# Attention in two passes, and the softplus polynomial by its quadratic factors, in a fused decoder layer

## The chip, the cores and the metric

The kernel runs on one core of one Trainium2 chip. The metric is the device time of one execution in microseconds (us). A difference counts here from 0.2% (about 3.3 us) on; the chances of the prediction are given by that bound. A profile is one execution taken by the hardware profiler.

## What is computed

One decoder layer over 4 batches of 512 tokens with 512 features, in fp32, in three parts, each added to the residual `x`:

```python
x = x + attention(layernorm(x))          # 16 query heads, 2 key/value heads, 32 features each, causal, rotary
x = x + mamba(ctx, gate=layernorm(x))    # selective scan, 512 channels, 16 states, z = layernorm(x)
x = x + ffn(layernorm(x))                # 1408 wide, silu gate, router, 8 adapters of rank 16, two chosen
```

The attention is `softmax(q @ k.T * scale, causal) @ v @ wo.T`. The scan, per state `n` of 16, is

```python
dt = softplus(w_dt @ (w_x @ u) + bias)                     # softplus(v) = relu(v) + log1p(exp(-abs(v)))
state = state * exp(dt * A[n]) + (dt * u) * B[n]           # along 512 tokens
y += state * C[n]
```

`log1p(t)` for `t` in 0 to 1 is `t` times a polynomial of degree 9.

## The kernel before, in words

All weights but those of the FFN stay in SBUF. The work of one batch is attention, the scan, then the FFN. The scan of batch t+1 does not depend on the residual, so its pieces are laid beside other work: beside the 33 evaluations of the FFN of batch t (gate and up, 11 tiles of 128 columns, three evaluations each), beside its down projection (11 tiles), and beside the 32 steps of attention of batch t+1. `plan` (L93) fills these slots in order: `PLAN_NEXT` gives the evaluations 30 pieces, the down projection 22 (`IN_DOWN`), attention the last 8. Batch 0 has no FFN before it, so `PLAN_FIRST` puts 13 pieces beside its projections and 47 into its attention. A state of the scan is three VectorE pieces over 128x2048 elements: `mul` (L1086), `run` (the scan itself, L1091) and `out` (L1096). For each state ScalarE makes the decay (four exponentials, L583) and fetches rows B and C (L573), and GpSimd adds the product to `y_sb` by an accumulating DMA (L487):

```python
pool.wait_ge(y_added, 16 * (b * NS + n))     # add n waits for add n-1
dve.wait_ge(y_added, 16 * (b * NS + n - 1))  # mul n (n >= 2) waits for add n-2: two state buffers
```

The softplus polynomial is the first 12 pieces: one TENSOR_SCALAR (L1061), nine SCALAR_TENSOR_TENSOR (L1064, Horner), the sum with relu (L1069), and `dt * u` (L1072).

Down projection (PE, L970 to L974): for each of 11 tiles four matmuls, and `project(b, f)` beside it (L774): in turn the raw q tiles and k (L782), their rotation (L789) and v (L796). `rotate` (L1098) on VectorE makes 3 instructions per tile, 5 tiles. `finish` (L1277) then adds the result out of the four banks of `ps_a`, and only then can attention use these banks.

Attention before has 32 steps: step s is two heads (`pair`) of query tile i (128 queries) against (i+1) key tiles. PE: two matmuls of 32 rows, side by side in the array, and two bf16 mask matmuls (`scores`, L820, L823). VectorE: negated row maxima (L1126). ScalarE: exponentials with bias and row sum (L625). PE: transposes of the probabilities (L834); ScalarE copies them to SBUF (L637). Each two steps make a group of four heads: PE spreads the inverse row sums (L844) and weighs the values (L849, four column tiles of 32 side by side), ScalarE and VectorE move and scale (L644, L1139). So each query tile passes PE, VectorE, ScalarE, PE, ScalarE, PE, ScalarE, VectorE. Two pairs of banks hold the scores: `scores(s)` waits for the exponentials of s-2. The output projection of query tile i (L873, four matmuls) comes at steps 31, 33, 34, 35 (`OUT_AT`). Then VectorE does the first sum (L1172), norm and gate (`gate_stages`, L1142).

Queues: SP loads inputs and FFN weights and stores the output; ScalarE's queue loads B and C; GpSimd's the accumulating DMAs and the small powers of the norms (L477). Matmuls in fp32 show as two records each (two passes), with two weight loads.

## Time and profile before

| | |
|---|---|
| Median of 3 runs | 1651.27 us (1648.47 to 1651.48) |
| Profiled execution: its own time | 1649.75 us |
| Its span, first to last instruction | 1647.9 us |
| Mean granted TensorE clock | 0.876 |
| Busy: PE, VectorE, ScalarE, GpSimd | 1406.0, 1218.4, 604.9, 111.9 us |

1649.75 us is the profiled execution's own time; the span leaves out what lies before the first and after the last instruction. Busy shares are averages over stages. PE's busy time counts matmuls in flight, so it grows when the clock is low.

The period of a batch in steady state is 384 us. In the trace the FFN of batch 0 and the scan of batch 1 lie between 293 and 541 us, the attention of batch 1 from 553.5 us, and so on.

### The profile page before, as it was taken

Reading aid. Unit: us, or ns where it says so; the run is one execution under the profiler, and the core shown is the slowest. Engines: PE = TensorE matmul, PEld = TensorE weight load, DVE = VectorE, ACT = ScalarE, POOL = GpSimd, SP = SyncE. Lnnn points to the kernel's source line nnn. Section 1 sums busy time; section 2 is a strip of 40 time slices with the busy share of each in tenths; the row PEclk is TensorE's granted clock in tenths of the full one; section 3 lists DMA queues with packets and bytes.
Section 4 is the critical chain, followed back from the end, with each engine's and each line's share of the span. In section 5 each row is a group of like instructions: output and inputs, shape, how many; then the busy total and the mean of one; then the engine's idle time right before and its main releaser. Section 6 shows DMA issues by size and latency. Waiting matters only on the chain.

```text
span 1647.9 us, 16148 instructions
## 1 busy us (share of the span) xinstructions
PE 1406.0 (85%) x5768; PEld 685.0 (42%) x5768; DVE 1218.4 (74%) x1411; ACT 604.9 (37%) x1436; POOL 111.9 (7%) x116
## 2 busy tenths in 40 slices
PE   5756767999888799899889699899879788799999
PEld 2333433443333354444334255444334345454434
DVE  4899996589989766759998865759998967623330
ACT  5165553323223584232232376242333267211110
POOL 0000001001100000000110000100210000100000
PEclk8855558999999699899999779899999869789999
DMA  4167761123666631112656822012556741101112
GB/s 185 39 147 153 154 141 27 44 66 108 143 141 166 166 66 26 39 50 78 159 128 159 196 68 52 26 37 84 124 131 152 173 135 27 26 13 64 48 32 83
DMA packets 53278, 158.81 MB, mean 96 GB/s; under 512 B 5072, under 2 KB 10704, under 8 KB 44752
## 3 DMA queue, kind: packets, MB, share of 16 engines
q0 software_dynamic: 9216, 67.11, 19.8%
q1 hardware_dynamic: 25664, 54.23, 9.9%
q10 hardware_dynamic: 18320, 36.45, 8.6%
q8 instruction: 47, 0.77, 0.2%
q14 instruction: 31, 0.25, 0.0%
HBM read 86.20 MB, written 4.46 MB: 55 GB/s over the span
## 4 chain that ended last, share of the span: by engine, by line
DVE 30%; issue 30%; PE 29%; DMA 6%; ACT 4%; POOL 2%; DVEq 0%; ACTq 0%; POOLq 0%
DVE state L1091 11%; DMA y_sb<-state 5%; PE ps_a L894 5%; DVE state L1086 4%; PE ps_a L974 4%; PE ps_a L820 3%; DVE state L1096 3%; PE ps_b L834 3%; PE ps_w L873 3%; PE ps_a L906 3%; POOL rstd L477 2%; PE ps_b L914 2%; PE ps_w L782 2%; ACT r L625 2%; DVE neg_max L1126 2%
## 5 line engine op out<-in xcount | busy, mean ns | idle before, releaser
L894 PE MATMUL ps_a<-xt,w_sb 128*128 128x512 f32 x704 | 319.2, 607 | 0.0
L1091 DVE TENSOR_TENSOR_SCAN state<-decay,state 128x2048 f32<-128x2048 f32 x64 | 282.8, 4418 | 5.3 <-ACT decay L583 0.5
L677 ACT ACTIVATE r<-ps_a 128x512 f32<-128x512 f32 x132 | 78.6, 596 | 380.6 <-PE ps_a L906 202.8
L894 PEld LDWEIGHTS ps_a<-xt,w_sb 128*128 128x128 f32 x704 | 138.1, 197 | 174.9 <-issue 174.9
L820 PE MATMUL ps_a<-r 32*128 32x512 f32 (+3 forms) x512 | 140.4, 634 | 81.7 <-ACT r L625 55.2
L906 PE MATMUL ps_a<-r,wb_sb 128*128 128x512 f32 x352 | 177.1, 628 | 35.9 <-DVE r L1267 33.7
L583 ACT ACTIVATE decay<-dt_sb,decay_rate 128x511 f32<-128x511 f32 x256 | 162.9, 712 | 104.9 <-DVE state L1096 72.2
L1260 DVE SCALAR_TENSOR_TENSOR r<-r,ps_a 128x512 f32<-128x512 f32 x132 | 89.9, 681 | 146.3 <-ACT r L677 146.3
L625 ACT ACTIVATE r<-ps_a,neg_max 128x128 f32<-128x128 f32 (+3 forms) x256 | 133.6, 534 | 116.6 <-DVE neg_max L1126 116.1
L974 PE MATMUL ps_a<-wd_sb,r 128*128 128x512 f32 x352 | 162.4, 613 | 0.0
L1086 DVE TENSOR_TENSOR state<-du_sb,bc_sb 128x2048 f32<-128x2048 f32 x64 | 146.3, 2286 | 4.7 <-DMA y_sb<-state 4.6
L1096 DVE TENSOR_TENSOR state<-state,bc_sb 128x2048 f32<-128x2048 f32 x64 | 145.9, 2280 | 0.7
L834 PE MATMUL ps_b<-cst,r 128*128 128x128 f32 x640 | 121.4, 333 | 26.0 <-ACT xt L637 16.8
L906 PEld LDWEIGHTS ps_a<-r,wb_sb 128*128 128x128 f32 x352 | 67.4, 197 | 131.1 <-issue 124.7
L1126 DVE TENSOR_REDUCE neg_max<-ps_a 128x2 f32<-128x256 f32 (+3 forms) x128 | 104.0, 814 | 21.1 <-PE ps_a L823 20.2
L487 POOL DMA_DIRECT2D y_sb<-state x64 | 56.1, 876 | 752.5 <-DVE state L1096 676.9
L974 PEld LDWEIGHTS ps_a<-wd_sb,r 128*128 128x128 f32 x352 | 70.1, 200 | 88.8 <-issue 86.8
L834 PEld LDWEIGHTS ps_b<-cst,r 128*128 128x128 f32 x640 | 89.9, 174 | 34.7 <-issue 29.5
L914 PE MATMUL ps_b<-r,ad_sb 128*128 128x512 f32 x176 | 89.8, 635 | 13.5 <-DVE r L1267 13.5
L820 PEld LDWEIGHTS ps_a<-r 32*128 32x128 f32 x512 | 49.9, 237 | 118.4 <-ACT r L625 77.2
L1267 DVE TENSOR_TENSOR r<-r,ps_a 128x512 f32<-128x512 f32 x132 | 90.7, 687 | 9.6
L477 POOL TENSOR_TENSOR rstd<-var_eps,cst 128x1 f32<-128x1 f32 x48 | 56.0, 1167 | 576.4 <-DVE var_eps L1024 576.4
(120 smaller groups left out, 1475.7 us busy)
## 6 DMA issues: line engine op xcount, KB each, us to landing
y_sb<-state POOLq DMA_DIRECT2D x64, 1024.0 KB, 9.7
bc_sb<-bc_rows ACTq DMA_DIRECT2D x64, 512.0 KB, 5.1
w_sb<-in_w_tiles SPq DMA_DIRECT2D x44, 512.0 KB, 3.7
wd_sb<-in_w_down SPq DMA_DIRECT2D x44, 256.0 KB, 3.5
wb_sb<-in_w_adapt SPq DMA_DIRECT2D x44, 128.0 KB, 2.1
xa<-in_x SPq DMA_DIRECT2D x4, 1024.0 KB, 5.2
out_x<-xb SPq DMA_DIRECT2D x16, 256.0 KB, 7.0
xn_att<-in_ctx_t SPq DMA_DIRECT2D x4, 512.0 KB, 6.1
```

Source lines behind the costliest of these rows:

```text
L583: nc.scalar.activation(decay[:, n % 2, j, 1:L], dt_sb[:, j, 1:L], ACT.Exp, scale=decay_rate[:, j, n:n + 1]).then_inc(decay_ready, 1)
L625: nc.scalar.activation(probs[:, (2 * s + k) % 4, 0:(i + 1) * P], score_place(s, k), ACT.Exp, bias=neg_max[:, s % 2, k:k + 1], accum_out=ro ...
L820: nc.tensor.matmul(score_place(s, k), q_t[rows, m, i * P:(i + 1) * P], k_t[rows, 0:width], start=True, stop=False, tile_position=(rows.sta ...
L834: mm = nc.tensor.transpose(ps_b[:, k, kt * P:(kt + 1) * P], probs[:, (2 * s + k) % 4, kt * P:(kt + 1) * P], ident)
L894: mm = nc.tensor.matmul(ps_a[:, 2 * (f % 2) + half, :], w_sb[:, slot, at + k * P:at + (k + 1) * P], xt[:, k, :], start=(k == 0), stop=Fals ...
L906: mm = nc.tensor.matmul(ps_a[:, 2 * (f % 2) + half, :], wb_sb[:, f % 2, at:at + P], low[:, 2 * half + k - 1, :], start=False, stop=(k == 2 ...
L914: mm = nc.tensor.matmul(ps_b[:, k - 1, :], ad_sb[:, f, :], hk[:, (2 * f + k - 1) % 4, :], start=(f == 0), stop=(f == FT - 1), skip_group_c ...
L974: mm = nc.tensor.matmul(ps_a[:, i, :], hb[:, f, i * P:(i + 1) * P], wd_sb[:, f % 2, :], start=(f == 0), stop=False, skip_group_check=True)
L1086: tt(state[:, n % 2, :, :], du_sb[:], row, ALU.mult).then_inc(scan_chain, 1)
L1091: nc.vector.tensor_tensor_scan(flat, decay[:, n % 2, :, :].rearrange("p j l -> p (j l)"), flat, 0.0, ALU.mult, ALU.add).then_inc(scan_chai ...
L1096: tt(state[:, n % 2, :, :], state[:, n % 2, :, :], row, ALU.mult).then_inc(scan_chain, 1)
L1126: nc.vector.tensor_reduce(neg_max[:, s % 2, :], both, AX.X, ALU.max, negate=True)\
```

## The change

Attention becomes two passes, both over 16 groups of four heads (one head tile m of four times one 128-token tile). Pass 1 only finds the row maxima: four score matmuls (four row tiles of 32, each into its own bank), masks, two maxima on VectorE per group. The maxima are then turned (four transposes) and copied once. Pass 2 makes the transposed scores, with keys on the partitions: k.T q, transposed mask, and a matmul of 32 rows that adds the negated maximum; ScalarE takes one exponential over two heads, without bias or sum; then PE weighs the values (no transposes) and sums the weights with a ones matmul. After all groups VectorE inverts the sums (two instructions 128x256), PE spreads them, VectorE divides (two of 128x1024), and the four output projections follow. Three pairs of banks hold scores. Three of the four q tiles are projected and rotated inside pass 1 instead of beside the down projection. No scan piece stands in pass 1; pass 2 has all that are left but for its last two groups. Three of the four input projections of the next batch's scan (L739) and their taps move ahead of the output projection.

The polynomial is written as `POLY[-1] * t * (t - r) * product of four ((t - a)^2 + c)`: ScalarE squares (with bias), VectorE multiplies by square + constant, on halves of 128x1024.

```diff
-NPOLY = len(POLY)
+POLY_LINE, POLY_PAIRS = quadratic_factors(POLY)
+QUADS = 2 * len(POLY_PAIRS)
+NPOLY = QUADS + 3
...
-IN_DOWN = 22 
+IN_DOWN = 13
+IN_MAXIMA = 0
-LAST_STEPS = 1
+LAST_STEPS = 2
-PLAN_FIRST = plan([0] * DOWN + EARLY_FIRST + spread_over(IN_DOWN_FIRST - sum(EARLY_FIRST), FT - 2) +
-                  spread_over(PIECES - IN_DOWN_FIRST, STEPS - LAST_STEPS) + [0] * LAST_STEPS)
+PLAN_FIRST = plan([0] * DOWN + EARLY_FIRST + spread_over(IN_DOWN_FIRST - sum(EARLY_FIRST), FT - 2) + [0] * GROUPS +
+                  spread_over(PIECES - IN_DOWN_FIRST, GROUPS - LAST_STEPS) + [0] * LAST_STEPS)
...
-    raw = f - 1 if 1 <= f <= TILES else None
-    back = f - 2 if 2 <= f <= TILES + 1 else None
-    return raw, back, {TILES + 2: 0, TILES + 3: 1}.get(f)
+    raw = f - 1 if 1 <= f <= 2 else None
+    back = f - 2 if 2 <= f <= 3 else None
+    return raw, back, {3: 0, 4: 1}.get(f)
+def group(g):
+    m, k = divmod(g, NT)
+    return m, NT - 1 - k, k
+def late_tile(g):
+    m, _, k = group(g)
+    return (m + 2, k) if m + 1 < MT and k < 3 else (None, None)
...
+            def square(b, k):
+                if k >= 2:
+                    act.wait_ge(poly_chain, b * NPOLY + k)
+                tiles = slice(k % 2 * JT // 2, (k % 2 + 1) * JT // 2)
+                nc.scalar.activation(square_sb[:, tiles, :], exp_v[:, tiles, :], ACT.Square,
+                                     bias=cst[:, C_ROOT + k // 2:C_ROOT + k // 2 + 1]).then_inc(square_ready, 1)
...
+                for n in range(GROUPS):
+                    exponents(n)
+                    if n > 0 and n % NT == 0:
+                        move_values(n // NT - 1)
+                    load_bc(b, slots[ATT + GROUPS + n])
+                    make_decay(b, slots[ATT + GROUPS + n])
...
+                for g in range(GROUPS):
+                    n, k = late_tile(g)
+                    if k in (0, 1):
+                        project_raw(b, n, range(2 * k, 2 * k + 2))
+                    if k == 2:
+                        rotate_raw(b, n)
+                    scores(g)
...
+                def weights(n):
...
+                    for j in range(HPT):
+                        nc.tensor.matmul(score_banks(STEPS + 2 * n + j // 2)[:, j % 2, 0:width],
+                                         k_t[head_rows(j), kt * P:(kt + 1) * P], q_t[head_rows(j), m, kt * P:L],
+                                         start=True, stop=False, tile_position=(j * HD, 0))
+                    for j in range(HPT):
+                        nc.tensor.matmul(score_banks(STEPS + 2 * n + j // 2)[:, j % 2, 0:P], ident_b[:], mask_t_b[:],
+                                         start=False, stop=False)
...
+                        mm = nc.tensor.matmul(score_banks(STEPS + 2 * n + j // 2)[:, j % 2, 0:width],
+                                              pick, max_rows[head_rows(j), kt * P:L],
+                                              start=False, stop=True, tile_position=(j * HD, 0))
+                def weigh_values(n):
...
+                    for j in range(HPT):
+                        mm = nc.tensor.matmul(values[head_rows(j), kt * P:L], v_sb[:, kt, j // 2 * HD:(j // 2 + 1) * HD],
+                                              probs_t[n % 2][:, j, 0:width], start=(kt == 0), stop=(kt == NT - 1),
+                                              tile_position=(0, j * HD), skip_group_check=True)
+                    for j in range(HPT):
+                        mm = nc.tensor.matmul(sums[head_rows(j), kt * P:L], ones[:, m, :],
+                                              probs_t[n % 2][:, j, 0:width], start=(n == 0), stop=(n == GROUPS - 1),
+                                              tile_position=(0, j * HD), skip_group_check=True)
...
+                turn_maxima()
+                weights(0)
+                for n in range(GROUPS):
+                    if n + 1 < GROUPS:
+                        weights(n + 1)
+                    weigh_values(n)
+                pe.wait_ge(exp_done, (b + 1) * STEPS)
+                for half in range(2):
+                    if b + 1 < BATCH:
+                        project_in(b + 1, [half])
+                    spread_inverse(half)
+                if b + 1 < BATCH:
+                    project_in(b + 1, range(2, XIN_EARLY))
+                for i in range(NT):
+                    project_out(b, i)
...
+                for g in range(GROUPS):
+                    n, k = late_tile(g)
+                    if k == 2:
+                        rotate_tile(b, n)
+                    maxima(g)
+                    for piece in slots[ATT + g]["dve"]:
+                        scan_piece(b, piece)
+                for n in range(GROUPS):
+                    for piece in slots[ATT + GROUPS + n]["dve"]:
+                        scan_piece(b, piece)
+                dve.wait_ge(pv_done, (b + 1) * GROUPS)
+                invert(0)
+                invert(1)
+                dve.wait_ge(pv_moved, (b + 1) * MT)
+                divide(0)
+                divide(1)
+                for i in range(NT + 2):
+                    gate_stages(i)
```

## Rows read from the trace of the kernel before

**Rows 1.** The page: busy time of the engines, share of the span, instructions

```profile
PE 1406.0 (85%) x5768; PEld 685.0 (42%) x5768; DVE 1218.4 (74%) x1411; ACT 604.9 (37%) x1436; POOL 111.9 (7%) x116
```

**Rows 2.** Stretches: length, busy PE, PEld, DVE, ACT, POOL us (records), granted clock, DMA share, GB/s

```profile
110.00:253.00 143.00, 95.33 (x652) 54.93 (x652) 139.32 (x107) 79.79 (x221) 12.29 (x14) 0.58 0.67 142
293.00:447.00 154.00, 144.99 (x335) 63.58 (x336) 126.26 (x147) 47.46 (x81) 13.51 (x8) 0.97 0.33 87
468.00:541.00 73.00, 65.98 (x151) 29.22 (x151) 65.65 (x38) 20.40 (x33) 4.35 (x5) 0.94 0.69 161
541.00:554.50 13.50, 4.46 (x14) 1.82 (x13) 13.30 (x8) 2.56 (x4) 1.73 (x2) 0.79 0.72 173
554.50:632.00 77.50, 70.92 (x678) 41.26 (x678) 53.62 (x83) 57.57 (x199) 1.74 (x2) 0.81 0.31 83
```

**Rows 3.** The same view, five microseconds each, from the start of attention of batch 1

```profile
553.00:558.00 5.00, 4.28 (x22) 2.37 (x22) 2.90 (x7) 1.86 (x10) 0.00 (x0) 0.50 1.03 228
...
578.00:583.00 5.00, 5.00 (x90) 3.63 (x94) 2.44 (x8) 4.49 (x21) 0.01 (x1) 1.00 0.87 192
```

**Rows 4.** Chain of waits, down projection of batch 0: start us, us, what

```profile
475.99 3.43 PE ps_w L782 x8
479.42 3.43 PE ps_a L974 x8
```

**Rows 5.** Chain of waits, attention of batch 1 and its output projection

```profile
582.25 0.36 PE ps_w L844 x8
582.61 0.87 PE ps_w L849 x32
583.48 0.84 PE ps_a L820 x4
584.32 0.22 PE ps_a L823 x2
...
634.50 3.63 PE ps_w L873 x8
...
653.73 0.61 DVE xa L1172
```

**Rows 6.** Groups: line, engine, operation, shapes, count | busy us, mean ns | idle before, releasers

```profile
L1126 DVE TENSOR_REDUCE neg_max<-ps_a 128x2 f32<-128x256 f32 (+3 forms) x128 | 104.0, 814 | 21.1 <-PE ps_a L823 20.2
...
L1091 DVE TENSOR_TENSOR_SCAN state<-decay,state 128x2048 f32<-128x2048 f32 x64 | 282.8, 4418 | 5.3 <-ACT decay L583 0.5 <-DVE state L1086 0.5
...
L583 ACT ACTIVATE decay<-dt_sb,decay_rate 128x511 f32<-128x511 f32 x256 | 162.9, 712 | 104.9 <-DVE state L1096 72.2 <-DVE state L1091 31.0 <-DVE decay L1074 1.8
...
L1096 DVE TENSOR_TENSOR state<-state,bc_sb 128x2048 f32<-128x2048 f32 x64 | 145.9, 2280 | 0.7
...
L637 ACT ACTIVATE xt<-ps_b 128x512 f32<-128x512 f32 x64 | 35.6, 615 | 16.5 <-PE ps_b L834 16.4
...
L1131 DVE RECIPROCAL row_inv<-row_sum 128x2 f32<-128x2 f32 x128 | 20.1, 157 | 9.8 <-ACT r L625 9.1
...
L1108 DVE TENSOR_TENSOR r<-ps_w,cst 128x512 f32<-128x512 f32 x20 | 13.7, 685 | 18.1 <-PE ps_w L789 18.0
...
L687 ACT ACT_TABLE_LOAD x1 | 1.3, 1283 | 3.6 <-issue 3.6
...
L1219 DVE RECIPROCAL rs<-rs 128x4 f32<-128x4 f32 x4 | 0.7, 178 | 0.1
```

**Rows 7.** Timeline, batch 0, VectorE: start us, us, engine, line, operation

```profile
40.25 20.90 DVE L1064 SCALAR_TENSOR_TENSOR du_sb<-du_sb,state 128x2048 f32<-128x2048 f32 x9
...
81.15 2.28 DVE L1086 TENSOR_TENSOR state<-du_sb,bc_sb 128x2048 f32<-128x2048 f32 x1
...
270.06 0.68 DVE L1172 TENSOR_TENSOR xa<-ps_w,xa 128x512 f32<-128x512 f32 x1
```

**Rows 8.** Last accumulating DMA of batch 0; issue to landing of all 64

```profile
250.34 0.88 POOL L487 DMA_DIRECT2D y_sb<-state  x1 [9.34 <-DVE state L1096]
...
DMA to landing us min/median/max: 6.9/9.7/12.1
```

More of the change, by code:

```diff
@@ L93, in plan @@
 def plan(counts):
-    pieces = [("poly", k) for k in range(NPOLY + 2)]
+    pieces = [("poly", k) for k in range(NPOLY)]
     for n in range(NS):
@@ L98, in plan @@
     assert sum(counts) == len(pieces), (sum(counts), len(pieces))
-    slots, at, k = [{"dve": [], "bc": [], "decay": [], "add": []} for _ in range(SLOTS)], {}, 0
+    slots, at, k = [{"dve": [], "bc": [], "decay": [], "add": [], "square": []} for _ in range(SLOTS)], {}, 0
     for s, count in enumerate(counts):
@@ L105, in plan @@
     for n in range(NS):
-        slots[between(at["poly", NPOLY - 4] if n < 2 else at["out", n - 2], at["mul", n])]["bc"].append(n)
-        slots[between(at["poly", NPOLY + 1] if n < 2 else at["run", n - 2], at["run", n])]["decay"].append(n)
+        slots[between(at["poly", NPOLY - 5] if n < 2 else at["out", n - 2], at["mul", n])]["bc"].append(n)
+        slots[between(at["poly", NPOLY - 1] if n < 2 else at["run", n - 2], at["run", n])]["decay"].append(n)
         slots[at["out", n]]["add"].append(n)
+    for k in range(2, QUADS):
+        free, used = at["poly", k - 1], at["poly", k + 1]
+        slots[between(free, used) if used > free else used]["square"].append(k)
     return slots
@@ L167, in uses_of @@
             names += [("xin", j) for j in range(XIN_EARLY)]
+        names += [("op", i) for i in range(NT)]
         names += [("yt", i) for i in range(NT)]
@@ L259, in decoder_layer @@
         xin_sb = relu_v
+        square_sb = dt_sb
         scrap = sb("scrap", [1, 1])
@@ L772, in xt_moved, with project_raw, rotate_raw @@
                     pe.wait_ge(work_free[bank], count + 1)
+            def project_raw(b, n, ks=range(KT)):
+                if ks[0] == 0:
+                    bank = fill(pe, ("raw", n), b)
+                bank = use(("raw", n), b)[0]
+                for k in ks:
+                    w = wq_sb[:, k, (n - 1) * P:n * P] if n > 0 else wk_sb[:, k, :]
+                    mm = nc.tensor.matmul(ps_w[:, bank, :], w, xt[:, k, :], start=(k == 0), stop=(k == KT - 1),
+                                          skip_group_check=True)
+                if ks[-1] == KT - 1:
+                    mm.then_inc(work_full[bank], 1)
+            def rotate_raw(b, n):
+                bank = fill(pe, ("back", n), b)
+                raw_bank, raw_count = use(("raw", n), b)
+                pe.wait_ge(work_free[raw_bank], raw_count + 1)
+                nc.tensor.matmul(ps_w[:, bank, :], rot, q_raw[:, n % 2, :], start=True, stop=True)\
+                    .then_inc(work_full[bank], 1)
             def project(b, f):
-                raw, back, values = projections(f)
+                raw, back, turn = projections(f)
                 if raw is not None:
@@ L798, in project @@
                     mm.then_inc(v_full, 1)
-                if values == 1:
+                if turn == 1:
                     pe.wait_ge(v_moved, b + 1)
```

422 lines of the change are left out of this document (218 added, 204 removed).

## The prediction

> **What bounds the kernel now.** I read the page first, for the busy shares: PE 1406.0 of 1647.9 us, VectorE 1218.4 [rows 1]. These are averages, so the stretches came next, to see which engine is full in which stage. Four readings matter. In the attention of batch 0 VectorE works 139.32 of 143 us, because 47 pieces of the scan lie there, and the clock is 0.58. Beside the FFN evaluations PE works 144.99 of 154 us. In the down projection PE and VectorE are both near full (65.98 and 65.65 of 73), and then PE works only 4.46 of 13.5 us while VectorE finishes late pieces before it can add the result. In the attention of batch 1 PE works 70.92 of 77.5 us and VectorE 53.62: PE bounds it, at a clock of 0.81 [rows 2]. Five microseconds at a time, that stage starts at a granted clock of 0.50 and is at 1.00 by 578 us [rows 3]. The chain of waits then gives PE's prices at the high level, and the groups those of VectorE and ScalarE.
>
> **The sum, batches 1 to 3.** One steady batch has two stretches that change: down projection (468 to 553.5 us, 85.5) and attention up to the last output projection (553.5 to 653.7, 100.2) [rows 2, 5].
>
> Down projection. Removed beside it: three raw tiles, three rotations, and 9 pieces of 22. PE keeps 11 tiles, two raw tiles, v and the last adapter step, 15 items of 3.43 us (51.5) [rows 4], two rotations of a quarter of that (1.7) and a turn of v (0.6, estimated from the rates of the transposes in these rows): 53.8 us. VectorE: five `run` (4.42), eight `mul` or `out` (2.28) [rows 6], two rotations of 3 x 0.69, and 2.4 for the adapter sum and v: 47 us, plus about 9 us in which the first rotation waits for PE. So both end near 522 to 525 us, `finish` (4 x 0.61, taken like the 0.61 of the first sum [rows 5]) at 527.5. Gain: 26 us.
>
> Pass 1. VectorE: maxima 104.0/4 = 26.0 us as before, the same shapes in 32 instructions, and three moved rotations, 6.2: 32.2. PE: per group 0.84 us of scores at 512 columns (0.21 per 128), four masks for 0.33 (two take 0.22) [rows 5]: 14 us in all, and three raw tiles and rotations, 12.9: 27. PE and VectorE take turns at being late inside a head tile (raw halves fall on the first two groups, the rotation on the third), and I add 3. At the low clock PE alone needs about 52. The stage begins after PE idles in `finish`, as it does now at 0.50, so I take 39; ends 34 and 52. ScalarE has 3 copies of 0.7.
>
> Pass 2. PE does four kinds of matmul per group, scores, maximum, values and sums, each at 0.21 us per 128 columns if four tiles run side by side (0.84 for a score step, 0.87 for 32 records of values) [rows 5]. The widths of a head tile are 4 + 3 + 2 + 1 times 128, so 0.213 x 4 x 10 x 4 head tiles = 34.1. Masks: 16 x 0.33 = 5.3. A change from one tiling to another costs about 0.14: eight records of spread inverses, which come first after transposes, take 0.36, and 32 of values behind them 0.87, or 0.22 for eight [rows 5]. Three further changes a group: 16 x 3 x 0.14 = 6.7. The turned maxima 0.5. PE 47. VectorE: 16 pieces, six `out`, five `mul`, five `run`: 47.2 us. They are held by the accumulating DMA: `mul` n waits for add n-2, with 9.7 us to landing [rows 8] and 0.4 to issue, so out 10 to out 15 ends 51 us after pass 1. ScalarE: 16 x 2 exponentials over a mean of 640 columns (512 take 0.615 [rows 6]; 0.73 estimated, 23), five decays of 4 x 0.71 (14), moves 3: 40, but a decay in front of an exponential delays PE some 1.5 us. Together: all sums done 54 us after pass 1 (51 to 75).
>
> Tail, all serial. Two reciprocals of 256 elements: 128x2 takes 157 ns and 128x4 178, so 10.5 ns an element, 2.8 us each [rows 6]; at 1.1 ns an element, as other operations go, it is 0.4. PE then has three input projections (moved from behind, 1.7 each), two spreads (16 column-tiled matmuls of 256, 1.7 each) and four output projections of 3.63 [rows 5]. The first spread starts at 2.8 and PE runs on: 2.8 + 4 x 1.7 + 14.5 = 24.1, and 0.2 for the handovers: 24.3 us (the first input projection is done before). The divisions (1.2 each, from 2.28 for 2048) fit in between. Before, three of four output projections overlapped the steps.
>
> Attention is 39 + 54 + 24.3 = 117.3 against 100.2: +17.1. The stretch after it keeps its 24.7 us.
>
> Polynomial. Nine operations of 2.32 us (20.90 for nine [rows 7]) and one of 1.22 become one of 2.3 and eight half ones of 1.2, the sum with relu keeps 2.3: VectorE saves 10 us a batch. But in batches 1 to 3 these lie in the first evaluations, where PE is full, and the plan fixes the number of pieces per evaluation, so nothing else moves up but one piece. Gain: 0; if that cover went, up to 10. ScalarE gets eight squares (about 1.03 us each, from 0.615 for 512); the first two stand between softplus and the next tanh: +1 us, 0 to 2.
>
> Per batch: -26 + 17.1 + 1 = -7.9; three: -23.7.
>
> SP's queue: the next context load now waits for the last q tile, inside pass 1, and the first FFN weights queue behind it; they are needed some 100 us later: 0. GpSimd's queue keeps its order.
>
> **Batch 0.** Here the order costs. Before, the first `mul` starts at 81.15 and the last add is issued at 250.34 us; the last first sum is at 270.06 [rows 7, 8]. After: the first polynomial operation 2 us later, ends near 56, two rotations instead of five, `mul` 0 and `run` 0 by 71. Then pass 1 (40) holds no piece: `out` 0 ends at 113. Fifteen more states follow at 9.7 us, the DMA's pace, as VectorE needs only 9.0: 259. The tail at a partly low clock, 26.6: 286. That is +16 (8 to 25).
>
> The Trainium skill states a rule that speaks against such passes: a change of tiling mode drains TensorE (TensorEngine Tiling, Key Properties). The trace agrees, with the 0.14 us a change already in the sum. The same skill has four row tiles side by side at 3.07 times one (TensorE: Matmul & The Clock Gate, Part 3); no row shows four, only two row tiles and four column tiles. By 3.07 four take 1.3 times one, so scores and maxima (34.1/2) take 5 us more in pass 2, an estimate from that page's figure.
>
> **Sum:** 1649.75 - 23.7 + 16 = 1642. The profiled execution is 1.5 us under the median, inside the spread of the runs, so I compare with 1650 to 1651.
>
> **Rivals.** A, *PE bounds both passes* (slower). Only pairs of row tiles are shown side by side; if four heads go two by two, scores and maxima cost 0.21 x 10 x 4 = 8.5 us more each time: pass 2 goes from 54 to 68, pass 1 gains 4 (27 to 35.5 against 32 plus waits): +18 a batch, 1642 + 54 = 1696. The same comes from a clock that stays at 0.5 for 20 us, as it does now at the start [rows 3]. For: no row has more than two row tiles at once. Against: column tiles do run four at a time (0.87 for 32 records). It decides from PE 5 us over VectorE's 51.
>
> B, *all hides* (faster): clock high at once (pass 1 34), pass 2 at 51, reciprocals at 0.4: 12.8 less a batch, 5 in batch 0: 1642 - 38 - 5 = 1599. For: pass 1 and 2 leave PE fewer waits than 32 dependent steps; against: the clocks of 0.58 and 0.81 in its attention stages [rows 2].
>
> C, *squares need another function table*: the profile shows no square, and one table load in the whole run, of 1283 ns [rows 6]. Two loads at each of seven places in a batch are 18 us of ScalarE, which is 47.46 of 154 us busy there [rows 2]; at most 10 of them would delay a tanh: 1642 + 3 x 10 = 1672.
>
> D, *nothing measurable*: the 26 us of the down projection are given back whole in attention and batch 0. That lies inside the forecast's own range.
>
> **How the numbers follow.** Forecast 0.50, own range 1625 to 1660 (faster 0.35, same 0.08, slower 0.07); A 0.27; B 0.13; C 0.05; 0.05 for another cause, split between same (0.02) and slower. Faster 0.48, same 0.10, slower 0.42. Both signs carry most of the chance; the predicted time is the forecast's. The range 1603 to 1698 takes in most of A and B.
>
> **What would show it.** From the start of the down projection to the last add of `finish` 59 us; pass 1 in 39 us with VectorE nearly full; four score records of one group starting within 0.1 us; VectorE waiting for y_sb in pass 2 rather than for PE; two reciprocals near 2.8 us; last first sum of batch 0 at 286 us. Wrong if PE is the one waited for throughout pass 2, if the clock stays at 0.5 in pass 1, or if batch 0 ends no later than 270.

## The result, and the profile after

The changed kernel takes 1686.53 us (median of four runs, 1678.55 to 1688.98) against 1651.38 for the kernel before in the same comparison: a ratio of 1.0207, with a 95% interval of 1.0171 to 1.0244. It is slower; 1642 was forecast, with 0.48 of the chance on faster and 0.42 on slower. The profiled execution took 1686.63 us, its span 1684.8, at a mean granted clock of 0.897 (0.876 before).

The page's first row of the changed kernel answers to [rows 1]:

```profile
PE 1407.9 (84%) x5912; PEld 620.1 (37%) x5912; DVE 1185.8 (70%) x1238; ACT 486.6 (29%) x781; POOL 112.5 (7%) x116
```

ScalarE lost 118 us of work and VectorE 33, PE nothing, and PE is the engine that fills most stretches. The stretches (columns as in [rows 2]) are, in order: batch 0 pass 1, pass 2 and tail; then evaluations of the first FFN, its down projection, pass 1, pass 2 and tail of batch 1; last the down projection ahead of batch 3.

```profile
73.40:118.00 44.60, 34.16 (x205) 14.32 (x205) 30.57 (x43) 6.26 (x10) 0.00 (x0) 0.77 0.14 53
118.00:268.60 150.60, 79.25 (x582) 29.14 (x581) 136.97 (x48) 56.31 (x91) 13.29 (x15) 0.66 0.70 154
268.60:294.90 26.30, 23.62 (x104) 10.04 (x104) 13.86 (x25) 3.79 (x6) 2.99 (x4) 0.88 0.20 40
...
319.00:494.90 175.90, 158.52 (x375) 69.38 (x376) 137.75 (x159) 64.11 (x103) 15.50 (x10) 0.97 0.36 93
494.90:558.20 63.30, 57.76 (x131) 25.16 (x130) 49.21 (x27) 9.62 (x15) 3.48 (x4) 0.96 0.64 149
558.20:606.70 48.50, 37.78 (x224) 15.57 (x222) 30.63 (x43) 2.06 (x3) 0.00 (x0) 0.82 0.19 60
606.70:660.40 53.70, 49.97 (x562) 20.40 (x561) 47.12 (x16) 34.67 (x56) 4.35 (x5) 0.97 0.65 139
660.40:685.30 24.90, 23.93 (x132) 10.41 (x124) 13.94 (x26) 5.65 (x9) 2.99 (x4) 1.00 0.21 43
...
1268.70:1338.10 69.40, 60.89 (x132) 26.35 (x131) 49.23 (x27) 9.61 (x15) 3.47 (x4) 0.90 0.58 138
```

In nearly every stretch PE is busy some nine tenths, or VectorE is (pass 2 of batch 0). The exception is pass 1, in which neither is: in batch 1 PE 37.78 and VectorE 30.63 of 48.5 us. By stage, in us, from the starts and ends of these groups in both traces:

| stage | before, batches 1 / 2 / 3 | after | forecast change |
|---|---|---|---|
| evaluations | 174.7 / 174.5 / 176.2 | 175.5 / 173.8 / 175.2 | +1 |
| down projection to last sum | 86.8 / 86.0 / 86.1 | 63.3 / 63.3 / 69.4 | -26 |
| attention | 99.8 / 100.5 / 100.7 | 127.0 / 127.0 / 123.3 | +17.1 |
| of it pass 1 | | 48.5 / 48.6 / 46.7 | (39) |
| of it pass 2 and tail | | 78.5 / 78.4 / 76.6 | (78.3) |
| to the next FFN | 24.1 / 22.4 / 24.5 | 21.9 / 22.2 / 24.6 | 0 |
| batch 0, to the next FFN | 293.0 | 319.4 | +16 |

Summed over the batches the error of the forecast is 45 us: pass 1 +27, down projection +15, batch 0 +10, evaluations -4, the stretch after attention -2, pass 2 and tail -1.

Three readings say where to look. First, pass 1 in steps of three microseconds:

```profile
573.00:576.00 3.00, 3.00 (x24) 1.18 (x16) 2.27 (x2) 0.38 (x1) 0.00 (x0) 1.00 0.00 0
576.00:579.00 3.00, 2.72 (x26) 1.02 (x18) 2.40 (x4) 0.30 (x1) 0.00 (x0) 1.00 0.00 0
579.00:582.00 3.00, 0.71 (x13) 0.59 (x13) 2.70 (x5) 0.00 (x0) 0.00 (x0) 1.00 0.00 0
582.00:585.00 3.00, 3.00 (x7) 0.88 (x4) 0.76 (x2) 0.00 (x0) 0.00 (x0) 0.54 0.00 0
585.00:588.00 3.00, 3.00 (x16) 1.33 (x16) 1.14 (x1) 0.00 (x0) 0.00 (x0) 0.89 0.00 0
...
597.00:600.00 3.00, 1.90 (x12) 0.86 (x12) 1.91 (x2) 0.00 (x0) 0.00 (x0) 0.50 1.01 402
600.00:603.00 3.00, 2.16 (x16) 0.86 (x12) 2.05 (x3) 0.00 (x0) 0.00 (x0) 0.50 0.06 21
```

The engines take turns. At 579 VectorE rotates a tile while PE works 0.71 us of three; then PE computes half a projection and VectorE works 0.76. And the granted clock is at 0.54 in the stretch after the one in which PE idled, so the projection VectorE waits for is also slow. Second, the waits of PE in the down projection ahead of batch 3 (engine, line, for what: us in total, times, longest):

```profile
PE ps_a L1069 <- DMA wd_sb<-in_w_down: 8.5, 2, 4.8
```

No such wait of PE is in the trace of before. Third, the groups (columns as in [rows 6]): the matmuls of the down projection, maxima, the new polynomial steps, the squares, the reciprocals.

```profile
L1069 PE MATMUL ps_a<-wd_sb,r 128*128 128x512 f32 x352 | 166.5, 628 | 19.7 <-DMA wd_sb<-in_w_down 19.7
...
L1230 DVE TENSOR_REDUCE neg_max<-ps_a 128x2 f32<-128x1024 f32 (+3 forms) x88 | 70.2, 821 | 44.5 <-PE ps_a L867 44.2
...
L1164 DVE SCALAR_TENSOR_TENSOR du_sb<-dt_sb,du_sb 128x1024 f32<-128x1024 f32 x32 | 38.2, 1220 | 4.8 <-ACT dt_sb L597 4.2
L597 ACT ACTIVATE dt_sb<-state,cst 128x1024 f32<-128x1024 f32 x32 | 35.7, 1142 | 5.6 <-DVE du_sb L1164 5.3
...
L1235 DVE RECIPROCAL r<-ps_b 128x256 f32<-128x256 f32 x8 | 13.5, 1725 | 2.2 <-PE ps_b L930 2.2
```

### The profile page after: what moved, and what is told of

Same layout as the page of the kernel before. It is cut to its first block, busy times and chain, and to the rows that moved or that the text cites. A ratio compares the mean times of both kernels' runs of the same rounds, so it can differ in the third digit from the quotient of the medians.

```text
span 1684.8 us, 15081 instructions
## 1 busy us (share of the span) xinstructions
PE 1407.9 (84%) x5912; PEld 620.1 (37%) x5912; DVE 1185.8 (70%) x1238; ACT 486.6 (29%) x781; POOL 112.5 (7%) x116
## 4 chain that ended last, share of the span: by engine, by line
PE 58%; DVE 24%; DMA 9%; ACT 4%; issue 3%; POOL 2%; DVEq 0%; ACTq 0%; POOLq 0%
PE ps_a L989 12%; PE ps_a L1069 9%; DVE state L1194 6%; DMA y_sb<-state 6%; PE ps_a L1001 5%; PE ps_w L812 4%; DVE state L1199 3%; PE ps_b L1009 3%; PE ps_w L968 3%; DVE neg_max L1230 3%; DMA wd_sb<-in_w_down 2%; DVE r L1365 2%; PE ps_a L863 2%; PE ps_w L771 2%; POOL rstd L509 2%
## 5 line engine op out<-in xcount | busy, mean ns | idle before, releaser
L1001 PE MATMUL ps_a<-r,wb_sb 128*128 128x512 f32 x352 | 175.1, 621 | 38.5 <-DVE r L1372 36.3
L710 ACT ACTIVATE r<-ps_a 128x512 f32<-128x512 f32 x132 | 78.5, 595 | 380.3 <-PE ps_a L989 196.4
L1069 PE MATMUL ps_a<-wd_sb,r 128*128 128x512 f32 x352 | 166.5, 628 | 19.7 <-DMA wd_sb<-in_w_down 19.7
L1001 PEld LDWEIGHTS ps_a<-r,wb_sb 128*128 128x128 f32 x352 | 66.5, 195 | 133.0 <-issue 127.1
L901 PE MATMUL ps_a<-r 32*128 32x384 f32 (+3 forms) x336 | 62.4, 553 | 54.4 <-ACT r L673 54.2
L1230 DVE TENSOR_REDUCE neg_max<-ps_a 128x2 f32<-128x1024 f32 (+3 forms) x88 | 70.2, 821 | 44.5 <-PE ps_a L867 44.2
L863 PE MATMUL ps_a<-r 32*128 32x512 f32 (+3 forms) x352 | 63.7, 578 | 26.5 <-DVE neg_max L1230 26.3
L812 PE MATMUL ps_w<-xt,wq_sb 128*128 128x512 f32 x128 | 69.2, 674 | 0.0
L643 ACT ACTIVATE r<-ps_w,q_bias 128x512 f32<-128x512 f32 x16 | 10.9, 684 | 199.6 <-PE ps_w L812 199.6
L673 ACT ACTIVATE r<-ps_a 128x512 f32<-128x512 f32 (+3 forms) x84 | 56.2, 693 | 40.9 <-PE ps_a L911 27.0
```

Source lines behind the costliest of these rows:

```text
L812: mm = nc.tensor.matmul(ps_w[:, bank, :], w, xt[:, k, :], start=(k == 0), stop=(k == KT - 1), skip_group_check=True)
L863: nc.tensor.matmul(score_banks(2 * g + j // 2)[:, j % 2, 0:width], q_t[head_rows(j), m, i * P:(i + 1) * P], k_t[head_rows(j), 0:width], st ...
L1001: mm = nc.tensor.matmul(ps_a[:, 2 * (f % 2) + half, :], wb_sb[:, f % 2, at:at + P], low[:, 2 * half + k - 1, :], start=False, stop=(k == 2 ...
L1069: mm = nc.tensor.matmul(ps_a[:, i, :], hb[:, f, i * P:(i + 1) * P], wd_sb[:, f % 2, :], start=(f == 0), stop=False, skip_group_check=True)
L1230: nc.vector.tensor_reduce(place, score_banks(2 * g + p)[:, :, 0:width], AX.X, ALU.max, negate=True).then_inc(neg_max_ready, 1)
```

## The experiments

Each time stands beside runs of the kernel before on the same chip. "Period" is the time from one FFN's first base matmul to the next one's.

### The two halves of the change by themselves

`poly_only` puts the factored polynomial into the kernel before; `old_poly` puts the old polynomial back into the changed one:

```diff
-NPOLY = len(POLY)
+NPOLY = QUADS + 3
...
-IN_DOWN = 22
+IN_DOWN = 21
```

```diff
-NPOLY = QUADS + 3
+NPOLY = len(POLY) + 2
...
-IN_DOWN = 13
+IN_DOWN = 14
```

> The kernel before with the factored polynomial alone (11 pieces instead of 12, squares on ScalarE, one piece less beside the down projection). Theory P (the polynomial gives VectorE 10 us a batch, but only batch 0, where VectorE is full, can use them): the first mul of batch 0 starts near 72 instead of 81.15 us, the scan's chain of adds starts as much earlier, batch 0 ends 7 to 10 us earlier, batches 1 to 3 change by -1 to +1 us each; total about 1642 us (1638 to 1647). Rival R (the squares stand in front of ScalarE's tanh and exponentials and cost more than they give): every evaluation stage 2 us or more longer, total 1652 to 1665 us. If the factored form were also worth its 10 us in the evaluations, the total would be 1612 to 1625.

Measured: 1637.17 us, ratio 0.9906 (0.9885 to 0.9927). The total is as theory P had it, but not the place. Batch 0 ends 1.9 us earlier, not 7 to 10. From 39 to 81 us, the stretch of the polynomial in batch 0, first of the kernel before, then of `poly_only`:

```profile
39.00:81.00 42.00, 30.98 (x74) 13.15 (x74) 36.65 (x29) 6.50 (x11) 0.00 (x0) 0.88 0.10 35
```

```profile
39.00:81.00 42.00, 33.20 (x84) 14.31 (x82) 30.84 (x31) 18.45 (x26) 0.00 (x0) 0.87 0.18 53
```

VectorE is 5.8 us less busy there. It starts 1.2 us later and once waits 4.1 us for ScalarE's squares, so the first `mul` starts at 76.9 instead of 81.15 us, not at 72. The larger part of the gain (8.5 of 12.8 us between the spans) lies beside the down projection, which has one piece fewer. From its start to the last sum in batch 1, first before, then `poly_only`:

```profile
467.70:554.50 86.80, 70.74 (x165) 31.34 (x163) 79.00 (x45) 23.26 (x37) 6.08 (x7) 0.91 0.69 163
```

```profile
466.40:549.80 83.40, 70.39 (x165) 31.30 (x163) 76.82 (x44) 21.60 (x34) 6.09 (x7) 0.93 0.72 160
```

There VectorE's pieces end last, so a piece of 2.3 us less gave 3.4, 2.6 and 2.5 us in the three batches. Attention became 0.5 to 1.6 us shorter as well, at a clock of 0.83 instead of 0.80. Rival R is refuted: evaluations are 175.5, 175.6 and 175.6 us against 174.7, 174.5 and 176.2.

> The changed kernel with the old polynomial (12 pieces, each over all 2048 columns). Theory P: VectorE's 10 us come back in batch 0 (first mul near 75 instead of 66.5 us, everything behind it as much later) and nearly nothing in batches 1 to 3: 1687 + 9 = 1696 us (1692 to 1700). Then two-pass attention with the old polynomial costs 45 us against the kernel before, not 35. Rival R (the squares are part of the loss): 1675 to 1686 us.

Measured: 1678.03 us, ratio 1.0159 (1.0142 to 1.0177). Wrong sign: in the two-pass kernel the new polynomial is 8 us slower than the old, though the intervals of the two ratios just touch (1.0142 to 1.0177, and 1.0171 to 1.0244). Batch 0 goes as P said in kind (1.5 us later), and 6.3 of the 7.2 us between the profiled spans lie in the period of batch 3. Its down projection with the old polynomial, which answers to the 69.40 us above:

```profile
1268.00:1330.20 62.20, 57.65 (x133) 24.89 (x131) 51.03 (x28) 11.43 (x18) 3.48 (x4) 0.97 0.67 162
```

PE waits 4.5 us for weights there instead of 8.5, and the clock is 0.97 instead of 0.90. The total lies in rival R's range, but not by R's cause: the evaluations, in which most of the squares stand, are as long as with them (173.2, 175.1 and 175.2 us). What differs is the wait for weight loads; `old_poly_third_wd` below tests that. With the old polynomial the two-pass attention alone costs 1.6%.

### Pass 1: order

`late_back` takes the late projections out of pass 1:

```diff
-    raw = f - 1 if 1 <= f <= 2 else None
-    back = f - 2 if 2 <= f <= 3 else None
+    raw = f - 1 if 1 <= f <= TILES else None
+    back = f - 2 if 2 <= f <= TILES + 1 else None
...
-    return (m + 2, k) if m + 1 < MT and k < 3 else (None, None)
+    return None, None
```

`scores_first` leaves them and changes the order, on PE as shown, on VectorE with `maxima(g)` ahead of `rotate_tile`:

```diff
+                    scores(g)
                     if k in (0, 1):
                         project_raw(b, n, range(2 * k, 2 * k + 2))
                     if k == 2:
                         rotate_raw(b, n)
-                    scores(g)
```

> The changed kernel with the projections and rotations of the last three q tiles back beside the down projection, as in the kernel before; pass 1 holds only scores, masks and maxima. Theory T (pass 1 is long because PE and VectorE take turns around the moved projections and rotations): in batch 0, where PE has room beside VectorE's polynomial, the maxima take 30 to 35 us instead of 44.6 and the batch ends 6 to 10 us earlier; in batches 1 to 3 pass 1 falls from 48.5 to 31 to 36 us, and the down projection grows from 63 by the 11 to 13 us of PE work moved into it; total 1670 to 1682 us. Rival C (the low clock at the start of the stage sets pass 1, whatever stands in it): pass 1 stays at 42 us or more, total 1690 to 1705 us.

Measured: 1692.01 us, ratio 1.0251 (1.0229 to 1.0272). Neither theory alone. The down projection grows by 8, 9 and 2 us; pass 1 falls to 41.3, 40.9 and 41.1 us (by 7, 8 and 6), with three projections and rotations gone from it. In batch 0 it takes 41.1 us, where theory T wanted 30 to 35, and its last first sum comes 3.4 us later instead of earlier. Pass 1 of batch 1:

```profile
567.40:608.60 41.20, 29.41 (x195) 13.32 (x195) 24.87 (x33) 0.00 (x0) 0.00 (x0) 0.58 0.19 62
```

Less work for PE, and the clock falls to 0.58; both engines are far from full, and it still takes 41 us. Rival C's total is in its range and its 42 us is missed by about one.

> The changed kernel with another order inside pass 1: PE issues the scores of a group ahead of the half projection or rotation that stood in front of them, VectorE takes the maxima of a group ahead of the rotation. The same instructions. Theory T (turns): each late maximum or score hides behind the other engine's own work; pass 1 falls from 48.5 to 38 to 42 us in batches 1 to 3 and from 44.6 to about 38 in batch 0, total 1687 - 3 x 8 - 6 = 1657 us (1648 to 1667). Rival C (clock, or PE's own work of 38 us with what it waits for the matmul before): the waits move to other instructions and pass 1 stays within 3 us, total 1675 to 1687 us.

Measured: 1672.02 us, ratio 1.0130 (1.0108 to 1.0153): -14 us. Pass 1 takes 43.2, 44.8 and 44.8 us (-5.3, -3.8, -1.9). In batch 0 it takes 45.0 us, no less than the 44.6 of the changed kernel. The FFN of that batch starts 3.7 us earlier all the same, but so it does in `next_in_pass1` below, which leaves batch 0 as it is; so these 3.7 us are not shown to come from the order. The order is part of the loss in batches 1 to 3, and less than theory T wanted. Pass 1 of batch 1:

```profile
552.80:596.00 43.20, 34.39 (x225) 15.04 (x225) 30.61 (x42) 2.06 (x3) 0.00 (x0) 0.89 0.22 67
```

### Pass 1: the clock

The question left was whether the low clock is a cause or only follows. The test is work whose result nobody reads: in `late_back_fill`, one matmul of 512 columns per group into a bank that is free there (for the first group PE first waits until both banks are).

```diff
                     scores(g)
+                    nc.tensor.matmul(ps_w[:, g % 2, :], ident, xt[:, g % KT, :], start=True, stop=True)
```

> The kernel with all projections beside the down projection (1692 us, pass 1 41 us at a granted clock of 0.52 to 0.58), plus one more matmul of 512 columns in each group of pass 1 whose result is never read: 64 matmuls more, nothing taken out. Theory K (with little work PE gets the low clock, and at the low clock its scores and masks are what VectorE waits for): the clock in pass 1 rises over 0.85, the maxima take 31 to 35 us instead of 41, and the total falls to about 1664 us (1656 to 1674) although PE does more. Rival U (the turns of two engines over three pairs of banks set the pace at any clock): pass 1 stays at 41 us or grows by up to 14, total 1692 to 1745.

Measured: 1665.13 us, ratio 1.0080 (1.0065 to 1.0096): 27 us faster than `late_back`, with 64 matmuls more and nothing removed. That is theory K, on its numbers. Pass 1 of batch 1:

```profile
560.30:594.20 33.90, 32.36 (x224) 12.96 (x225) 24.98 (x34) 0.00 (x0) 0.00 (x0) 1.00 0.22 76
```

The clock goes from 0.58 to 1.00 and the pass from 41.2 to 33.9 us; in the other batches, batch 0 too, it gets 7.1 to 7.4 us shorter.

The same idea on the kernel before, in `poly_only` with nine matmuls ahead of the first scores:

> The kernel before with the factored polynomial (1637 us), plus 9 matmuls of 512 columns in batches 1 to 3 between the end of the down projection and the first scores, whose results are never read. In poly_only PE idles there for 8.5 us, and the granted clock is then 0.50 from 545 to 570 us. Theory K (idle time of PE is paid a second time, in the low clock behind it): the attention stage starts at a clock of 1.00 and is 4 to 9 us shorter in each of three batches, total 1637 - 18 = 1619 us (1610 to 1626). Rival L (in the one-pass attention the chain from scores over exponentials to transposes sets the pace at any clock): total 1633 to 1642.

Measured: 1640.15 us, ratio 0.9934 (0.9911 to 0.9958), within its error `poly_only`'s time. K failed here. The end of the down projection and the start of attention, first `poly_only`, then with the nine matmuls:

```profile
538.00:549.00 11.00, 1.67 (x6) 0.64 (x6) 10.83 (x7) 2.56 (x4) 0.86 (x1) 0.75 0.75 162
549.00:570.00 21.00, 20.01 (x92) 9.87 (x95) 12.34 (x20) 13.68 (x45) 0.00 (x0) 0.50 0.62 187
```

```profile
538.00:549.00 11.00, 9.57 (x26) 4.04 (x24) 10.83 (x7) 2.55 (x4) 0.86 (x1) 1.00 0.72 163
549.00:570.00 21.00, 19.32 (x96) 9.54 (x98) 12.52 (x20) 13.78 (x45) 0.00 (x0) 0.54 0.61 188
```

Most of the gap was filled and the clock held at 1.00 to 549, but it was at 0.54 over the next 21 us all the same. Rival L's time came out, but L was not tested, since the clock stayed low. What PE did just before the clock fell, at 550.6 us, from the last of the nine matmuls on (timeline; in brackets the idle time before, and who ended it):

```profile
545.45 1.88 PE L840 MATMUL ps_w<-xt,cst 128*128 128x512 f32 x4
548.76 0.49 PE L852 MATMUL ps_a<-r 32*128 32x128 f32 x4 [1.43 <-DVE xb L1321]
...
549.96 0.49 PE L852 MATMUL ps_a<-r 32*128 32x128 f32 x4 [0.48 <-DVE xb L1321]
```

The nine matmuls end 1.4 us too early, and the first score steps leave PE idle again. So here work ahead of the stage did not carry its clock, while work in the gaps of the stage did in `late_back_fill`. A fill in the gaps of the one-pass attention was not run. Why the clock stays at 0.54 with PE busy 19.32 of 21 us, no run here says.

`after_fill` then put ten such matmuls a batch into the changed kernel alone, behind the scores of the third and fourth group of each head tile and in each group of the last:

```diff
+                    if m == MT - 1:
+                        bank = g % 2
+                    elif k >= 2:
+                        bank = use(("raw", m + 2), b)[0]
...
+                    nc.tensor.matmul(ps_w[:, bank, :], ident, xt[:, g % KT, :], start=True, stop=True)
```

> The changed kernel, nothing moved, with 10 matmuls more a batch whose results are never read: one behind the scores of the third and fourth group of each head tile, and one in each group of the last, where the trace has PE idle and the granted clock at 0.5 to 0.8 just behind. Theory K (this idle time is what lowers the clock, and the low clock is part of the 9.5 us by which pass 1 was mis-sized): clock in pass 1 from 0.82 to over 0.93, pass 1 from 48.5 to 42 to 45 us, total 1687 - 15 = 1672 us (1665 to 1678). Rival T (pass 1 is long by the order of its work alone): the matmuls cost PE 8.6 us a batch in front of the next scores, total 1687 to 1705.

Measured: 1675.57 us, ratio 1.0128 (1.0101 to 1.0156): -11 us, near the edge of K's range. Pass 1, then pass 2 with the tail:

```profile
558.00:602.60 44.60, 39.32 (x241) 15.76 (x240) 30.66 (x43) 2.06 (x3) 0.00 (x0) 1.00 0.20 65
602.60:680.70 78.10, 72.91 (x689) 30.66 (x687) 60.87 (x40) 40.34 (x65) 7.34 (x9) 1.00 0.50 109
```

The clock is 1.00 in both and pass 1 takes 44.5 us in all three batches, although it holds 8.6 us more of PE work. So at least 4 of the 9.5 us by which pass 1 was too long were clock (in batch 3, 2 of 7.7). The total gained less than it might have: the down projection of batch 1 took 69.7 us instead of 63.3, with PE waiting for its weights again. The run also shows PE's own work at the high level: 39.3 - 10 x 0.86 = 30.7 us, where the forecast had 27.

The Trainium skill describes this pattern (TensorE: Matmul & The Clock Gate, A second HAM failure mode: psum-queue depth-cycling): short idle times between groups that cycle through PSUM banks make the clock swing. The trace agrees, with clocks of 0.50 to 0.89 behind the gaps of pass 1.

### The scan in pass 1

`first_in_pass1` puts 16 of batch 0's pieces into pass 1, `next_in_pass1` 8 of batches 1 to 3:

```diff
-                  spread_over(PIECES - IN_DOWN_FIRST, GROUPS - LAST_STEPS) + [0] * LAST_STEPS)
+                  spread_over(16, GROUPS) +
+                  spread_over(PIECES - IN_DOWN_FIRST - 16, GROUPS - LAST_STEPS) + [0] * LAST_STEPS)
```

```diff
-IN_MAXIMA = 0
+IN_MAXIMA = 8
```

> The changed kernel with 16 of the 46 remaining scan pieces of batch 0 put into pass 1 (one a group), which was empty of them; 30 stay in pass 2. Theory E (batch 0 loses 24 us because the scan and its chain of adds stand still for the 45 us of pass 1): the last first sum of batch 0 comes 8 to 25 us earlier than 294.9 us, total 1675 us (1662 to 1679). Rival H (a piece ahead of a maximum holds PE up, the granted clock falls, and both passes give it back): batch 0 within 4 us of 294.9, total 1683 to 1690.

Measured: 1667.35 us, ratio 1.0092 (1.0067 to 1.0118): -19 us, theory E. The last first sum of batch 0 ends at 275.0 us instead of 294.9. Pass 1 and pass 2 of batch 0:

```profile
73.40:148.10 74.70, 40.59 (x205) 17.18 (x205) 73.17 (x58) 13.92 (x22) 4.55 (x5) 0.59 0.56 130
148.10:248.90 100.80, 63.07 (x581) 24.58 (x581) 92.06 (x32) 46.38 (x75) 8.77 (x10) 0.80 0.70 152
```

VectorE is full in pass 1 (73.17 of 74.7), against 30.57 of 44.6 in the changed kernel. The clock of 0.59 can have cost little there, since VectorE idled only 1.5 us.

> The changed kernel with 8 scan pieces of batches 1 to 3 moved from pass 2 into pass 1. VectorE is busy 30.6 of 48.5 us in pass 1 and 47.1 of 53.7 in pass 2, PE 37.8 and 50.0. Theory V (pass 2 is bound by the scan's pieces and adds, as the forecast had it): pass 2 falls by 10 us or more to PE-free waits, pass 1 grows by 6, total 1670 to 1680. Rival W (PE is what fills pass 2, at 50 of 53.7 us): pass 2 falls by 3 us at most, pass 1 grows by 8 to 12, total 1698 to 1713.

Measured: 1736.73 us, ratio 1.0526 (1.0486 to 1.0567): 50 us slower, worse than rival W. Pass 1, then pass 2 with the tail, of batch 1:

```profile
565.30:626.10 60.80, 38.20 (x224) 16.43 (x222) 50.06 (x49) 9.39 (x15) 2.61 (x3) 0.77 0.38 95
626.10:704.80 78.70, 73.76 (x686) 30.77 (x685) 40.81 (x33) 33.16 (x53) 4.73 (x6) 0.98 0.30 65
```

Pass 2 and tail take 78.7 us with VectorE busy 40.8, and took 78.6 with 61.1 (the other batches 81.6 and 75.2, against 78.4 and 76.6). So PE sets them, and what moves out of them buys nothing, while pass 1 grows by 12 to 15 us. PE's waits for down-projection weights also rose, from 19.7 to 25.3 us in all: the down projection of batch 1 took 73.0 us instead of 63.3, with nothing moved in it.

### The weights of the down projection

```diff
-        wd_sb = sb("wd_sb", [P, 2, D])
+        wd_sb = sb("wd_sb", [P, WD, D])
-                if f >= 2:
-                    sp.wait_ge(wd_used, t * FT + f - 1)
+                if f >= WD:
+                    sp.wait_ge(wd_used, t * FT + f - WD + 1)
```

> The changed kernel with three places instead of two for the tiles of the down projection's weights, so that each load starts one tile (3.4 us) earlier. Theory D (without the q projections between its tiles the down projection outruns its loads, which take 6.5 to 8.5 us beside an accumulating transfer; it waits 19.7 us in three batches, and the granted clock is 0.50 for about 4 us after the longest waits): the waits of PE for these weights fall under 3 us, the down projection to 56 to 58 us in each batch instead of 63.3, 63.3 and 69.4, total 1665 us (1658 to 1670). Rival S (the transfers share full DMA engines, so an earlier load is only a slower one, or VectorE's pieces end the stage anyway): total 1680 to 1688.

Measured: 1675.27 us, ratio 1.0140 (1.0121 to 1.0159): -11 us, between the two. The stage does nearly as theory D says, 60.1, 60.7 and 59.6 us, and PE waits for no weights. The first (with half a microsecond ahead of it) and the last:

```profile
491.20:551.80 60.60, 56.34 (x134) 24.61 (x132) 48.91 (x27) 9.61 (x15) 3.48 (x4) 1.00 0.66 152
...
1263.10:1322.70 59.60, 55.80 (x133) 24.44 (x131) 48.93 (x27) 9.62 (x15) 3.48 (x4) 1.00 0.65 151
```

The clock is 1.00 in both. Of the 15 us that the stages lose together some came back in attention of batch 1, 130.3 us against 127.0.

> The changed kernel with the old polynomial and three places for the down projection's weights. Two runs stand against each other: on the kernel before the factored polynomial gains 15 us, on the changed kernel it costs 8. Theory D (in the changed kernel its one piece less shifts the adds onto the weight loads, which then hold PE up for 19.7 instead of 13.4 us, with low clock behind): with the loads early the order turns round, and the old polynomial is the slower one by 1 to 6 us, 1676 to 1681 us against the 1675 of the run with three places. Rival Q (the squares themselves cost the two-pass kernel time): the old polynomial stays ahead, 1664 to 1670 us.

Measured: 1686.39 us, ratio 1.0221 (1.0202 to 1.0240). With the loads early the old polynomial is the slower one, by 11 us, in the direction of theory D but twice its size. Rival Q is refuted. Something else remains: the third place made the old-polynomial kernel 8 us slower. Its pass 1 takes 50 us at a clock of 0.77, against 47.0 at 0.83 with two places, with the same records in it:

```profile
559.20:609.30 50.10, 39.28 (x221) 16.09 (x221) 30.62 (x42) 2.06 (x3) 0.00 (x0) 0.77 0.21 61
```

```profile
557.80:604.80 47.00, 36.15 (x221) 15.04 (x221) 30.60 (x42) 2.06 (x3) 0.00 (x0) 0.83 0.21 66
```

What decides when the clock falls was not settled. Kernels that differ only ahead of pass 1 differ in it by 3 us in batch 1.

### Parts put together

`mix_c` is the changed kernel with `third_wd`, `first_in_pass1`, the order of `scores_first` from the second group on, and four idle matmuls in the last head tile. `two_pass_best` is `late_back_fill` with the first two. `mix_d` is `mix_c` with the idle matmuls of `after_fill` and the whole third projection ahead of the first scores.

> The changed kernel with four edits together: three places for the down projection's weights (measured -11 us), 16 scan pieces of batch 0 in pass 1 (-19), scores and maxima ahead of projections and rotations except in the first group (-14), and four idle matmuls in the last head tile of pass 1, where no projection is left. If the parts add up, 1687 - 44 = 1643 us, and 3 to 6 us less for the last: 1638 us (1630 to 1646). If they hide each other, because each only removes a wait that another one replaces: 1650 to 1665.

Measured: 1642.27 us, ratio 0.9950 (0.9932 to 0.9968). The parts add up nearly whole (44 us of 48).

> The kernel with all projections beside the down projection and a matmul more in each group of pass 1 (1665 us), with three places for the weights and 16 scan pieces of batch 0 in pass 1. If they add up (batch 0 -19; weights -6, for PE still waits 3 x 2.6 us there): 1640 us (1634 to 1647). If the pieces in pass 1 of batch 0 hold PE up as the projections did: 1650 to 1660.

Measured: 1649.93 us, ratio 0.9992 (0.9976 to 1.0009). Slower than the 1634 to 1647 expected. Batch 0 brought 15 us, the third place nothing: with projections between the tiles the down projection stays at 72.0 us (71.3 to 72.9 before it), and the trace of `late_back_fill` has no wait of PE for these weights that it could remove. Pass 1 became 2 us longer in each batch, at a clock of 0.93.

> The run with four edits (1642 us), with the idle matmuls of after_fill, and the whole projection of the third q tile ahead of the first scores, where PE waited 2.5 us for the last sum. Theory K: the clock in pass 1 goes from 0.86 to over 0.95, pass 1 from 45.4 to 36 to 40 us, total 1642 - 3 x 7 = 1621 us (1612 to 1628). Rival T: pass 1 stays at 44 us or more, total 1638 to 1650.

Measured: 1634.06 us, ratio 0.9893 (0.9872 to 0.9914). Pass 1 takes 41.5, 42.2 and 41.4 us, between both theories, at a clock of 0.96 (0.92 in batch 2). Its total lies between theirs too. It beats both kernels, as `poly_only` does (0.9906); their intervals overlap, so the runs don't rank them. Pass 1 and the rest of attention in `mix_d`:

```profile
533.70:575.20 41.50, 38.18 (x234) 15.89 (x235) 30.74 (x43) 1.52 (x3) 0.00 (x0) 0.96 0.23 75
575.20:653.40 78.20, 72.92 (x689) 30.66 (x687) 60.85 (x40) 40.34 (x65) 7.34 (x9) 1.00 0.50 109
```

## Why the prediction was wrong

**Pass 1 was the step that failed.** VectorE at 32.2 us, PE at 27, 3 added for taking turns, all taken as 39 for the clock, measured 48.5. VectorE's term was about right (30.6).

PE's term was 3.7 short (30.7 at the high level), by a misread row. The 0.84 us of [rows 5] were priced as "scores at 512 columns", but that step has 384. The same records in the timeline of before, which has the columns:

```profile
583.41 0.91 PE L820 MATMUL ps_a<-r 32*128 32x384 f32 x4
```

And a step of four heads over 512 columns in the changed kernel, in the timeline and in the chain of waits:

```profile
634.19 1.14 PE L901 MATMUL ps_a<-r 32*128 32x512 f32 x8
...
634.26 1.07 PE ps_a L901 x8
```

At the high clock four row tiles take 0.44, 0.65, 0.86 and 1.07 us for 128, 256, 384 and 512 columns: 0.21 per 128 columns, as forecast, and 0.22 on top. Over 16 groups the 0.22 come to 3.5 us.

The 3 us for turns was a token where the term should have been worked out group by group. What is left is turns (the order: 2 to 5 us a batch) and the clock those turns bring (4 us or more), and the two can't be added, because a gap is paid as a gap and again as slow work behind it. The forecast saw the clock of 0.50 at the start of the old attention [rows 3] and named "if the clock stays at 0.5 in pass 1" among what would make it wrong. It expected the low clock at the start, however, and there the clock is at 1.00 up to 567 us; it falls inside the pass. This step is 27 of the 45 us.

**Down projection, -26 a batch.** The end of the stage was sound: with a third place for the weights it measures 60.1, 60.7 and 59.6 us against the forecast's 59.5, with PE busy 56 where 53.8 was forecast. The step left out is the feed. Before, raw tiles and rotations stood between the tiles, and the load of the next but one had time; at 3.43 us a tile it doesn't always: these loads land after 2.4 to 3 us where no add is in flight, and up to 8.5 us after their issue beside one. Cost: 3 us in two batches, 10 in batch 3. The forecast counted the queues of SP and GpSimd for order, not for time. 15 us.

**Batch 0, +16, measured +24 at the last first sum (294.9 us, forecast 286) and +26 at the start of the FFN.** The start was nearly right: `mul` 0 at 66.5 us, `run` 0 ended at 73.5 against 71, with 4.2 us of waiting for a square in the polynomial. So were the states at the DMA's pace (9.89 us each, forecast 9.7). Pass 1 was 44.6 instead of 40, and from there `out` 0 ends at 120.2 instead of 113. The named reason, that the scan stands still during pass 1, is shown by `first_in_pass1`: 19 us of the total. Its first FFN starts at 297.8 us, in kernels that leave batch 0 as it is at 315.7 to 319.4.

**Pass 2: right number, wrong bound.** 54 us forecast, 53.7 measured. But it was put down to VectorE and the accumulating DMA at 51 with PE at 47; PE takes 50.0 (the 32 sets of row tiles cost 32 x 0.22 = 7.0 us more than priced, beside the 6.7 us put in for changes of tiling), and `next_in_pass1` shows that a third less VectorE work changes nothing. "VectorE waiting for y_sb" in pass 2 is not there.

**Tail.** 24.3 forecast, 24.9 measured. A reciprocal of 256 elements takes 1.73 us, not 2.8; the estimate from [rows 6] divided a time that is mostly fixed by two elements. PE runs on, so it did not matter.

**Rival A** is refuted in its first mechanism. Four row tiles do run side by side, started within 0.02 us of each other. The chain of waits in pass 2 at the high clock, with start, us and records: scores, masks and maxima over 384 columns, then values and sums over 512.

```profile
625.05 0.93 PE ps_a L901 x8
625.98 0.33 PE ps_a L905 x4
626.30 0.86 PE ps_a L911 x8
627.16 0.99 PE ps_b L924 x8
628.16 0.86 PE ps_b L930 x8
```

Four row tiles of 384 columns take 0.86 us where two take 0.84 in [rows 5]. Its time, 1696, is nearer to the result than the forecast's. Its other cause, a low clock, is nearer to what happened: the clock costs time in pass 1, though by falling inside it and not by staying at 0.5 for 20 us at its start. By the Trainium skill (TensorE: Matmul & The Clock Gate, Part 3) four row tiles come to 3.07 times one. The trace nearly agrees: a projection takes 3.43 / 4 = 0.86 us for one matmul of 512 columns over the whole array, and four row tiles of 512 columns take 1.07 us, so 3.2 times.

**Rival B** did not happen: a reciprocal of 1.73 us lies between its 0.4 and the forecast's 2.8, and the clock was high at once but did not stay. **Rival C** is refuted: evaluations changed by +0.8, -0.7 and -1.0 us with squares in them, and the trace still has one table load. **The polynomial** was costed at 0 in batches 1 to 3 with one piece moving up; alone in the one-pass kernel it takes 2.5 to 3.4 us a batch from the down projection, since that piece was among those that ended the stage last. In the two-pass kernel the factored form is 8 us behind (`old_poly`), and 11 us ahead once the weight loads are early (`third_wd` against `old_poly_third_wd`).

## What to carry to other kernels

Two engines that hand small tiles to each other can make a stage longer than either's work; lay the stage out group by group, and ask which other work can stand in its gaps. Where PE's granted clock falls behind its own gaps, matmuls whose result nobody reads can pay for themselves; here they did inside those gaps and not ahead of the stage. Before the price of a record is scaled by its width, read its width in the timeline. And when work is taken from between the uses of a streamed weight, check that its load still fits in the time that is left, beside the transfers that run there.

## What the runs showed of the hardware

- Added work shortened a program: 64 matmuls more, 27 us less, the clock of pass 1 from 0.58 to 1.00 (`late_back_fill`).
- A stage entered at a clock of 1.00 was at 0.54 over its first 21 us all the same, after PE had idled 1.43 and 0.48 us (`one_pass_fill`).
- At the high clock four row-tiled fp32 matmuls side by side take 1.07 us for 512 columns and 0.44 for 128; two take 1.06 and 0.42, and one matmul of 512 columns over the whole array 0.86. Four column tiles of 512 columns take 0.86 too.
- A reciprocal of 128x256 takes 1.73 us, 6.7 ns an element, where a multiplication of 128x2048 takes 2.29 us, 1.1 ns an element.
